# A transformer layer on one core: seven routed experts computed densely, or on 70 gathered tiles of 128 rows

## The reference

```python
x = x + attention(layernorm(x))            # 16 heads, bias by distance
xf = layernorm(x)                          # 4096 rows of 256
sh = gelu(xf @ sw1 + sb1) @ sw2 + sb2      # shared expert, every row
logits = xf @ gate_w.T + expert_bias       # 7 routed experts
topv, topi = top_k(logits, 2)
w = softmax(topv)
combine = sum(one_hot(topi, 7) * w[..., None], axis=1)
h = gelu(einsum('td,edh->eth', xf, rw1) + rb1[:, None, :])
out_e = einsum('eth,ehd->etd', h, rw2) + rb2[:, None, :]
x = x + sh + einsum('te,etd->td', combine, out_e)
```

## Time and profile before

| | us |
|---|---|
| median of 3 runs (lowest, highest) | 989.52 (987.48, 989.68) |
| the profiled execution | 985.09 |
| its span, first to last instruction | 983.3 |
| TensorE busy | 931.1 (95%) |
| VectorE busy | 708.1 (72%) |
| ScalarE busy | 501.3 (51%) |
| GpSimd busy | 109.4 (11%) |
| mean granted clock of TensorE | 0.969 of 2.4 GHz |

### The profile page before, as it was taken

The page is one execution under the profiler, slowest core; times in us unless marked ns, Lnnn a source line. Parts: engine busy times, 40 slices in busy tenths (PEclk is TensorE's granted clock), DMA queues, the critical chain, the costliest instruction groups (busy, mean ns, idle before and its releaser), DMA issues. The chain is left out here.

```text
span 983.3 us, 20280 instructions
## 1 busy us (share of the span) xinstructions
PE 931.1 (95%) x7264; PEld 695.4 (71%) x7264; DVE 708.1 (72%) x2048; ACT 501.3 (51%) x680; POOL 109.4 (11%) x245
## 2 busy tenths in 40 slices
PE   5799689999999999999996799999999999999998
PEld 3688366666666666666663588989888888888887
DVE  5566588888888888888854686666666666657664
ACT  2344136666666666666674553434434434444342
POOL 2111011111111111111110010000101010100100
PEclk9999669999999999999998899999999999999999
DMA  4998855434543454333513321102020111100000
GB/s 117 297 333 307 246 122 138 126 110 133 149 124 110 132 150 126 109 109 101 173 56 125 90 75 30 57 1 87 2 82 5 43 43 43 43 22 22 1 23 21
DMA packets 65715, 100.27 MB, mean 102 GB/s; under 512 B 11256, under 2 KB 39440, under 8 KB 65598
## 3 DMA queue, kind: packets, MB, share of 16 engines
q1 hardware_dynamic: 62386, 97.49, 32.6%
q0 software_dynamic: 3072, 1.11, 0.8%
q10 hardware_dynamic: 172, 0.56, 0.2%
HBM read 63.67 MB, written 34.93 MB: 100 GB/s over the span
## 5 line engine op out<-in xcount | busy, mean ns | idle before, releaser
L672 DVE CUSTOM_DVE_ANT_0 sums<-pS,near 128x512 bf16<-128x512 f32 x512 | 329.2, 687 | 52.0 <-PE pS L732 43.8
L703 ACT ACTIVATE prob<-pE 128x1024 f32<-128x1024 f32 x256 | 248.4, 1021 | 152.3 <-PE pE L757 152.2
L1182 PE MATMUL pD<-w2p,h_p 128*128 128x256 f32 x1536 | 203.1, 285 | 1.8 <-DVE x L1032 1.8
L1182 PEld LDWEIGHTS pD<-w2p,h_p 128*128 128x128 f32 x1536 | 191.4, 188 | 11.3 <-DVE x L1032 2.6
L1164 PE MATMUL pU<-x2T,w1p 128*128 128x512 f32 x768 | 189.5, 396 | 0.0
L1095 ACT ACTIVATE h_f<-pU,b1s 128x512 f32<-128x512 f32 x128 | 88.2, 689 | 190.0 <-PE pU L1164 184.4
L757 PEld LDWEIGHTS pE<-bandT,place 64*128 64x128 f32 x2048 | 166.3, 190 | 12.2
L757 PE MATMUL pE<-bandT,place 64*128 64x244 f32 (+2 forms) x2048 | 163.5, 272 | 0.0
L1164 PEld LDWEIGHTS pU<-x2T,w1p 128*128 128x128 f32 x768 | 140.1, 188 | 28.8
L1032 DVE SCALAR_TENSOR_TENSOR x<-pD,combine,x 128x256 f32<-128x256 f32 x256 | 110.8, 478 | 64.1 <-PE pD L1182 62.4
L732 PE MATMUL pS<-k_st,q_st 48*128 48x512 f32 x512 | 139.8, 477 | 10.7 <-DVEq L658 7.6
(11 more groups left out here) (102 smaller groups left out, 597.5 us busy)
## 6 DMA issues: line engine op xcount, KB each, us to landing
x<-in_x SPq DMA_DIRECT2D x16, 512.0 KB, 4.2
q_parts<-qk SPq DMA_DIRECT2D x16, 512.0 KB, 4.6
k_parts<-qk SPq DMA_DIRECT2D x16, 512.0 KB, 4.6
q_st<-q_parts SPq DMA_DIRECT2D x64, 128.0 KB, 2.7
k_st<-k_parts SPq DMA_DIRECT2D x64, 128.0 KB, 2.9
ctx<-ctx_sb SPq DMA_DIRECT2D x32, 256.0 KB, 2.7
near<-bias_by_distance SPq DMA_DIRECT2D x16, 448.0 KB, 5.3
v_rows<-vs SPq DMA_DIRECT2D x8, 512.0 KB, 3.2
```

What stands on the lines that cost most here:

```text
L672: dve.tensor_tensor_reduce(sums[:, r % 4], pS[:, unit % PS], near[:, hg % 2, j, lead:lead + S], -1.0, BIG, ALU.add, ALU.min, nmax[:, j, t: ...
L703: act.activation(prob[:, par, 2 * step:2 * step + 2], pE[:, 2 * (step % 2):2 * (step % 2) + 2], ACT.Exp).then_inc(exp_done, 1)
L1182: ins = pe.matmul(pD[:, t2, u], h_p[:, e % 2, a, m, P * t:P * t + P], w2p[:, e, z, m], start=k == 0 and e < NE - 1, stop=k == 5)
```

## The change

The shared expert stays dense: 12 and 24 matmuls per batch, and the bias matmuls. The seven routed experts are no longer run on every row.

In a first part, which runs over the eight batches, each batch's rows are normalised into `xr` (by ScalarE, twice, one copy for each of the row's two experts, with the destination row and the weight appended as two more values: 258 values), and a rank is computed for each row within its expert (a matmul with a triangular matrix, a running count per expert on VectorE). GpSimd scatters the rows with eight indirect DMAs per batch (128 rows of 1032 bytes each) into DRAM, `routed_rows`, sorted by expert. Seven more indirect DMAs write padding rows so that every expert's stretch ends on a multiple of 128. VectorE works out a table: for each of 70 tiles its first row and its expert.

In a second part, SyncE reads the first row of each tile into a register and loads the tile (8 buffers). TensorE transposes it, reads the expert's number into a register, runs six matmuls of 256 columns with the weights addressed by it, VectorE adds the bias (also by a register), ScalarE applies Gelu, TensorE transposes the hidden rows, reads the expert's number again and runs six more. VectorE scales by the row's weight, and GpSimd scatters the result by an indirect DMA to `expert_rows` in DRAM. The two high/low splits per tile are on ScalarE and VectorE as before.

In a third part SyncE loads the two results of every row (1 MB per batch), VectorE adds them, and the batches are stored. The shared expert runs for batches 0 to 4 inside the first part, for batch 5 while the table is made, for batches 6 and 7 (`HELD` on) in this last part.

The product of context and inverse denominators and the low part of the context move from VectorE to GpSimd, `normalise` from VectorE to ScalarE. All eight batches of x stay on the chip (`x1c`). There are no loops left in `finish`.

The constants and SyncE's block:

```diff
+XW = D + 2
+NXG, NY = 8, 4
+NT = 2 * B * S // P + NR - 1
+LAST, HELD = 5, 6
...
+                sp.wait_ge(s["tab_done"], 2)
+                for par in range(2):
+                    sp.wait_ge(scat[par], 16 * 2 * TT * (B // 2))
+                sp.wait_ge(pad_out[0], 16 * NR)
+                sp.wait_ge(pad_out[1], 16)
+                for i in range(NT):
+                    if i >= NXG:
+                        sp.wait_ge(y_out[i % NXG], 16 * (i // NXG))
+                    row = sp.value_load(table[0:1, 0, i:i + 1], min_val=0, max_val=NE * RS - P)
+                    sp.dma_start(xg[:, i % NXG], xs_dram[bass.ds(row, P), :]).then_inc(xg_ld[i % NXG], 16)
+                for k in range(NXG):
+                    sp.wait_ge(y_out[k], 16 * len(range(k, NT, NXG)))
...
+                for b in range(B):
+                    sp.wait_ge(s["y_acc"], b + 1)
+                    if b + 2 < B:
+                        load_rows(b + 2)
+                    sp.dma_start(g["out_t"][b], x1v(b)).then_inc(st, 16)
```

GpSimd's block:

```diff
+                context(0)
+                inverse_deviation(0)
+                context(1)
+                for i in range(B):
+                    if i + 1 < B:
+                        inverse_deviation(i + 1)
+                    if i + 2 < B:
+                        context(i + 2)
+                    scatter(i)
...
+                for e in range(NR):
+                    pool.indirect_dma_start(xs_dram[:, :], bass.IndirectOffsetOnAxis(ap=pad_i[:, e:e + 1], axis=0),
+                                            pad[:, e], None).then_inc(pad_out[0], 16)
+                for i in range(NT):
+                    pool.wait_ge(s["ev_done"], i + 1)
...
+                    pool.indirect_dma_start(yc_dram[:, :], bass.IndirectOffsetOnAxis(ap=place_of, axis=0),
+                                            y_sb[:, i % NY], None).then_inc(y_out[i % NXG], 16)
```

The order of VectorE's work, first and second part:

```diff
+                for i in range(B):
+                    if i + 1 < B:
+                        residual(i + 1)
+                    gate(i)
+                    if 1 <= i <= LAST:
+                        low(i - 1)
+                    choose(i)
+                    running(i)
+                    if 1 <= i <= LAST:
+                        add(i - 1)
+                    if i + 1 < B:
+                        lows(i + 1)
+                    slots(i)
+                    for k in (2 * i, 2 * i + 1):
+                        weights_lo(k)
...
+                for k in range(-4, NT):
+                    if k + 4 < NT:
+                        x_low(k + 4)
+                    if 0 <= k + 1 < NT:
+                        h_low(k + 1)
+                    if k >= 0:
+                        evict(k)
+                    if 0 <= k + 3 < NT:
...
+                        bias(k + 3)
```

ScalarE's, the same two parts:

```diff
+                for i in range(B):
+                    if 1 <= i <= LAST:
+                        shares(i - 1)
+                        hidden(i - 1)
+                    if i + 1 < B:
+                        normalise(i + 1, 0)
+                    soft(i)
...
+                    if k + 4 < NT:
+                        x_high(k + 4)
+                    if 0 <= k + 1 < NT:
+                        h_high(k + 1)
+                    if 0 <= k + 3 < NT:
+                        gelu(k + 3)
```

TensorE's routed up product, and the order of its second part:

```diff
+                def expert_up(i):
+                    expert = pe.value_load(table[0:1, 1, i:i + 1], min_val=0, max_val=NE - 1)
+                    pe.wait_ge(s["xlo"], i + 1)
+                    if i >= 2:
+                        pe.wait_ge(s["ub_done"], i - 1)
+                    for k, (c, (a, z)) in enumerate((c, hl) for c in range(MC) for hl in HL):
+                        ins = pe.matmul(pU[:, i % 2, 0:HID], xgT[:, i % 2, a, P * c:P * c + P],
+                                        w1p[:, bass.ds(expert, 1), z, c].rearrange("p a n -> p (a n)"), start=k == 0, stop=k == 5)
+                    ins.then_inc(s["up_mm"], 1)
...
+                for k in range(-4, NT):
+                    if k + 4 < NT:
+                        turn_tile(k + 4)
+                    if 0 <= k + 1 < NT:
+                        turn_hidden(k + 1)
+                    if k >= 0:
+                        expert_down(k)
+                    if 0 <= k + 3 < NT:
+                        expert_up(k + 3)
```

More of the change, by code:

```diff
@@ L941, in residual, with lows @@
                         dve.bn_aggr(mv[:, t], stats[:, t]).then_inc(s["var2"], 1)
[L943 to L949 removed]
+                def lows(b):
                     for c in range(MC):
@@ L1066, in _ @@
-                low(0, 0)
-                pairs(dve, batch)
+                    numbers = number[:].unsqueeze(1).to_broadcast([P, TT, NE])
+                    for c in range(2):
+                        ins = dve.tensor_tensor(picks[:, c], numbers, at[:, :, c].unsqueeze(2).to_broadcast([P, TT, NE]),
+                                                ALU.is_equal)
+                        ins.then_inc(s["chosen"], 1)
+                    count = count + 2
+                    dve.wait_ge(s["chosen"], count)
@@ L1069, in _ @@
+                for b in range(HELD, B):
+                    low(b)
+                    gather_add(2 * (b - HELD))
+                    gather_add(2 * (b - HELD) + 1)
+                    add(b)
+                for b in range(2 * (B - HELD), B):
+                    gather_add(b)
             @block.scalar
@@ L1100, in batch @@
-                def batch(b, par, i, first, last):
-                    for e in range(NE):
-                        if not (last and e == NE - 1):
-                            hidden(NE * b + e + 1, (e + 1) % NE, first and e == 0)
-                        if e == 4:
-                            act.wait_ge(s["c_turn"], b + 1)
-                            act.activation(cTs[:], pX[0:3 * NE, 1], ACT.Copy).then_inc(s["cT_done"], 1)
-                        if not last:
-                            mix(b + 1, 1 - par, e)
-                        for k in LATE.get(e, ()) if first else ():
-                            weights_hi(k)
+                    act.activation((w1p, w2p)[k % 2][:, e, 0], wst[:, k % WS], ACT.Copy).then_inc(s["w_hi"], 1)
@@ L1122, in _ @@
+                for b in range(LAST, HELD):
+                    shares(b)
+                    hidden(b)
+                for k in range(-4, NT):
[5 more added lines that the diff above has]
+                        gelu(k + 3)
+                for b in range(HELD, B):
+                    shares(b)
+                    hidden(b)
             @block.tensor
```

782 lines of the change are left out of this document (515 added, 267 removed).

## The result

The changed kernel took 1011.2 us (median of 4 runs, 1010.5 to 1012.9) beside 989.6 us for the kernel before on the same chip: a ratio of 1.022, 95% interval 1.020 to 1.025. The forecast was 1000. So it is slower, in the direction and in the range forecast, by 22 us instead of 10. The profiled execution has a span of 1009.8 us, 16.5 more than the 993.3 forecast for it.

What follows compares the result with a forecast made beforehand. The prediction took TensorE's matmul columns to bound the expert stage. Routing to 711.4, tiles to 948.2 and the end gave a span of 993.3 against 983.3, so 989.5 + 10 = 999.5, say 1000 us; range 938 to 1078.

Steps and rivals of the forecast that it cites:

- What bounded the kernel before, and what was removed: Expert stage, 454.8 us: bound by TensorE's matmul columns; 317.5 us removed, 139 added back, 179 saved, all lost to idle time.
- Routing: First part, from 528.5 us: normalising, choosing and scattering eight batches, with the first tile at 711.4.
- one loop sets the pace: Routing rounds: scatters, GpSimd's inverse deviation, ScalarE's normalise, tanh, VectorE's choice and slots follow one another, 19.5 us a batch.
- Slots of batch 0: Start of the first part: first slots ready 38.3 us into the stage, at 566.8.
- third rival: GpSimd in the first part: an indirect DMA costs 1.5 us, not 0.9; 38 us more, 1038; chance 0.16.
- Behind the last slots: End of the first part: eight scatters 7.2, padding 6.3, landing 3.0, SyncE's load of the first tile, from 691.2 to 711.4.
- TensorE's 14 us a round: First part: TensorE's own work per batch, about 14 us, lies beside the 19.5 us loop.
- The tiles: Second part: TensorE's 1.98 us plus two exposed register loads of 0.6 make 3.2 a step; 74 steps, 236.8 us.
- first rival: Second part: TensorE's queue hides the register loads, VectorE's loop of 2.6 us sets the step; 44 us less, 955; chance 0.30.
- The end: Third part: last scatter and landing 3.9, 12.6 MB by DMA at 333 GB/s 37.8, last store 2.9 us.
- second rival: Second part: TensorE stays at 1.2 GHz through the tiles; 126 us more, 1126; chance 0.11.

Runs made afterwards that it cites:

- twelve scatters: The changed kernel with four of each batch's eight scatters issued once more, into rows that nobody reads: 1048.7 us, ratio 1.061.
- split scatters: The changed kernel with GpSimd's inverse deviation of batch i+2 between the fifth and sixth scatter of batch i: 1027.9 us, ratio 1.038.
- context on VectorE: The changed kernel with the context's product and subtractions moved from GpSimd back to VectorE: 1013.8 us, ratio 1.025.
- slots first: The changed kernel reordered on TensorE, VectorE and ScalarE so that a batch's slots wait for nothing of the next batch: 1009.9 us, ratio 1.022.
- copy early alone: The changed kernel with only ScalarE's copy of the context moved ahead of the next batch's turned copy and second normalisation: 1018.8 us, ratio 1.030.
- Slots first with the context on VectorE: The changed kernel with slots not waiting for the next batch, and context product and subtractions on VectorE behind lows(i+1): 1014.7 us, ratio 1.028.
- Slots first with the copy early: The changed kernel with slots not waiting for the next batch and ScalarE's context copy moved ahead; context stays on GpSimd: 992.2 us, ratio 1.003.
- the run of 983.8: The changed kernel with slots not waiting for the next batch, ScalarE's context copy early, and context work on VectorE before the slots: 983.8 us, ratio 0.996.

## Why the prediction was off

**What bounded the kernel before, and what was removed**: right. TensorE's busy time fell, by 114 us and not 179, and idle time took back more than all of it, as forecast.

**Routing: the failed step.** The forecast says: "From there one loop sets the pace", with a round of 19.5 us, and put the first tile at 711.4. It came 44 us later:
- Slots of batch 0: 574.4 instead of 566.8, 8 us. The product over 1024 values, put at 1 us or more, took 2.39 on GpSimd.
- Rounds: from batch 0 to 7 they took 154 us instead of 124, 30 us. Of that, the price of an indirect DMA is 48 x (1.27 - 0.9) = 18 us, 3.0 in each of six rounds (the last, from batch 6 to 7, has no scatter in it: 8.5 us, forecast 8.8). That is the third rival's mechanism at 1.27 in place of its 1.5, and the twelve scatters show it on the chain. The other 12 us come from the path: the chain ran through ScalarE's second normalisation, its turned copy, its copy of the context and GpSimd's 3.0 us of subtractions. The forecast never put these on it, though it had moved the subtractions to GpSimd ahead of the scatters. That is 1.4 us in a steady round, 23.9 - 19.5 less the 3.0, and more in the first two.
- The forecast also took the scatter buffer to be free in time. It was part of a second loop of nearly the same length. Edits that opened one loop gave nothing (split scatters, context on VectorE, slots first, copy early alone). Slots first with the context on VectorE opened both and built a third, and gave nothing either. Slots first with the copy early gave 19 us, and 27 with the context on VectorE.
- Behind the last slots: 26.8 us instead of 20.2, of which 15 indirect DMAs at 0.37 are 5.6.
- TensorE's 14 us a round, put beside the loop at full clock, were 15.9 in the round shown above (649.65 to 673.52 us), at a granted clock of 0.86. They lay nearly beside the loop there: the turned rows started 0.9 us behind the end of the normalisation that they wait for (669.25 and 668.33). How much the lower clock took from the gain of shorter waits isn't shown.

**The tiles**: the mechanism was right (register loads stand exposed, TensorE sets the step, the full clock returns), the size was not. The term was 0.6 us a load; they measured 0.50 and 0.38, and the rest of TensorE's step was 1.9. The step was 2.79 instead of 3.2, 33 us less in all. The first rival's loop of 2.6 us was real, 2.48, and became the bound as soon as one load was gone.

**The end**: 51 instead of 45. The DMAs ran at 219 to 291 GB/s, not 333, and VectorE waited for the held shared batches at half clock. Without these batches the end was 46 us, so they account for at most 5 us of it. Holding them back saves 23 us ahead of the tiles.

**The first rival** (hidden loads, a step of 2.6) didn't come: both loads were exposed.

**The second rival** (half clock in the tiles): wrong there, 0.98. But the half clock came in the two parts around the tiles, in which TensorE waits for others.

Two errors of opposite sign, +44 + 6 and -33.5, left 16.5 of the span. Of the median's 22 us against 10 they leave 12, since the forecast had added 4.4 us for a profiled execution below its median, and the changed kernel's (1011.6) lay on it. That the time came out closer than its parts is luck.

## What to carry to other kernels

When work is taken off the bounding engine, draw the chain of one round through all engines and through the buffers, with every instruction that stands ahead in an engine's order, since what set such a stage here was the order of the work and not its amount on any engine. Look for a second loop before you pay for opening the first: here four single edits changed the time by +17 to -1 us, and two of them together by -19. Load a register once per tile and keep it: the second load on TensorE cost 21 us of 1011. And look for the same row in the traces of other kernels before you blame an edit or the clock for a few us: a stop of 3 us a round stood in the traces of one chip alone.

## What the runs showed of the hardware

- An indirect DMA of 128 rows of 1024 or 1032 bytes holds GpSimd 0.96 us, and the next comes 0.30 later (64, 7 and 70 of them; the first of a row takes 1.10 to 1.50). Landing takes 2.7 us from the issue for the results of the tiles, one at a time (median), and in rows of eight 2.4 to 6.2, median 3.8 (the round of 612 to 636 us in the run of 983.8).
- A register load from SBUF on TensorE wasn't hidden by the matmuls ahead of it: 0.50 and 0.38 us of idle time, with the register operations behind it, before the first weight load that uses it; 0.43 for the one that was left.
- VectorE was held up by GpSimd. Its mask on 128x32 took 2.36 us beside GpSimd's product on 128x1024 (2.38) and 0.19 without it; a cast on 128x8 took 1.07 instead of 0.17 beside GpSimd's subtractions. The Trainium skill says in SBUF — State Buffer, "Who interferes with whom", that a VectorE instruction with two inputs in SBUF contends with a GpSimd instruction that reads SBUF, and that a cast can contend too. These rows agree. It cost about 3 us a round, which gave nothing back when it went (context on VectorE), since another loop was about as long.
- In routing, where TensorE waited 2 to 6 us at a time for other engines, the rows show a mean granted clock of 0.69 to 0.86, a mixture of 2.4 and 1.2 GHz; in the tiles, with waits of 0.2 to 0.5 us, 0.98.
- GpSimd takes 2.38 us for the product of 128x1024 and 3.01 for two subtractions of 128x512; VectorE took 1.23 and 1.29.
